# Moving two VectorE operations later in each step of a cross-attention and routing pipeline

## The reference

```python
# x: (32, 100, 256), ctx: (32, 361, 192)
x1 = layernorm(layernorm(x)) * g1 + b1            # two norms in a row
x2 = layernorm(ctx) * g2 + b2
q, k, v = x1 @ Wq + bq, x2 @ Wk + bk, x2 @ Wv + bv
attn = softmax(q @ k.T * E ** -0.5)               # row maximum subtracted
x = x + (attn @ v) @ Wo + bo

h = layernorm(x)                                  # 3200 tokens
shared = gelu(h @ ws1 + bs1) @ ws2 + bs2
aff = softmax(h @ Wr + br)                        # 31 experts
vals, idx = top_k(aff, 3)
routed = sum over the 3 experts e of vals_e * (gelu(h @ We1[e] + Be1[e]) @ We2[e] + Be2[e])
x = x + shared + routed + h
```

## Time and profile before

| | us |
|---|---|
| median of 3 runs | 512.76 |
| lowest, highest | 511.71, 514.05 |
| the profiled execution | 512.76 |
| its span | 511.0 |

### The profile page before, as it was taken

How to read it: one execution, slowest core, us unless ns; L and a number is a source line. 1 busy time by engine, 2 the same in 40 slices (tenths; PEclk the granted TensorE clock), 3 DMA queues, 4 the chain that set the end, 5 groups by cost and what they waited for, 6 DMA issues and landing times.

```text
span 511.0 us, 13549 instructions
## 1 busy us (share of the span) xinstructions
PE 461.7 (90%) x3204; PEld 407.2 (80%) x3204; DVE 350.6 (69%) x1556; ACT 247.2 (48%) x821; POOL 324.9 (64%) x363
## 2 busy tenths in 40 slices
PE   1899888889798989988899999999999999999992
PEld 1777777778677778767799889999999999999891
DVE  4747878887878887657467666666666666661684
ACT  1255655556465654656355454555554545552220
POOL 6123756857576755747078888888888888885000
PEclk9989999999999997999999999999999999999997
DMA  7374876767575972568369999998888888875999
GB/s 242 101 215 126 243 224 196 247 206 244 182 236 175 347 250 75 192 212 314 97 133 181 187 189 182 182 153 140 137 136 140 135 139 135 138 115 79 331 349 325
DMA packets 80621, 97.53 MB, mean 191 GB/s; under 512 B 8689, under 2 KB 65298, under 8 KB 80546
## 3 DMA queue, kind: packets, MB, share of 16 engines
q1 hardware_dynamic: 60786, 70.79, 45.8%
q0 software_dynamic: 19472, 25.61, 30.0%
q10 hardware_dynamic: 288, 0.27, 0.3%
HBM read 54.91 MB, written 41.73 MB: 189 GB/s over the span
## 4 chain that ended last, share of the span: by engine, by line
PE 45%; DVE 16%; DMA 9%; issue 9%; POOL 5%; SPq 4%; ACT 2%; POOLq 0%; DVEq 0%
PE bank L1184 12%; PE bank L1195 11%; DMA sum<-y_sb,token 7%; PE bank L1173 3%; DVE w_all L732 3%; POOL sum L557 2%; PE bank L1085 2%; PE bank L1086 2%; DMA w_all<-sum 2%; PE bank L1039 2%; PE bank L1051 2%; PE bank L1040 1%; SPq L449 1%; DVE c L695 1%; DVE y_sb L790 1%
## 5 line engine op out<-in xcount | busy, mean ns | idle before, releaser
L557 POOL DMA_INDIRECT sum<-y_sb,token x105 | 170.3, 1622 | 47.3 <-issue 24.6
L643 ACT ACTIVATE up<-bank,b_all 128x128 f32<-128x128 f32 x260 | 81.4, 363 | 102.0 <-PE bank L1184 65.8
L1184 PE MATMUL bank<-xtt,w1b 128*128 128x128 f32 x840 | 111.1, 275 | 0.3 <-ACT xtt L669 0.3
L1195 PE MATMUL bank<-w_all,up 128*128 x420 | 108.5, 381 | 0.0
L1184 PEld LDWEIGHTS bank<-xtt,w1b 128*128 128x128 f32 x840 | 102.1, 192 | 0.7 <-ACT xtt L669 0.5
L921 DVE TENSOR_SCALAR y_sb<-bank,gate,inverse 128x256 f32<-128x256 f32 x105 | 57.1, 544 | 55.1 <-PE bank L1195 54.9
L535 POOL DMA_INDIRECT expert_rows_in<-xt,slot x75 | 76.2, 1016 | 21.0 <-issue 20.7
L1195 PEld LDWEIGHTS bank<-w_all,up 128*128 128x128 f32 x420 | 71.7, 191 | 5.7 <-issue 0.2
L913 DVE COPY w1b<-w_all 128x512 f32 x105 | 47.8, 455 | 16.7 <-PE bank L1184 5.9
L669 ACT ACTIVATE xtt<-bank 128x256 f32<-128x256 f32 x105 | 40.1, 383 | 38.7 <-PE bank L1173 38.1
L1173 PE MATMUL bank<-ident,xt 128*128 128x128 f32 x210 | 40.1, 273 | 0.3 <-DMA xt<-expert_rows_in 0.3
(11 more groups left out here) (180 smaller groups left out, 935.4 us busy)
## 6 DMA issues: line engine op xcount, KB each, us to landing
xt<-expert_rows_in SPq DMA_DIRECT2D x105, 132.0 KB
w_all<-in_w SPq DMA_DIRECT2D x47, 256.0 KB, 5.0
w_all<-in_ctx SPq DMA_DIRECT2D x32, 288.0 KB, 3.0
w_all<-sum SPq DMA_DIRECT2D x15, 384.0 KB, 7.5
sum<-pad_rows SPq DMA_DIRECT2D x1, 3328.0 KB, 12.7
w_all<-in_x SPq DMA_DIRECT2D x25, 128.0 KB, 3.3
sum<-y_sb SPq DMA_DIRECT2D x25, 128.0 KB, 3.5
sum<-xt SPq DMA_DIRECT2D x25, 128.0 KB, 3.4
```

The source lines that it names most:

```text
L557: pool.indirect_dma_start(sums[s], bass.IndirectOffsetOnAxis(ap=token[sx][:, 0:1], axis=0), y_sb[sx][:, :], None, compute_op=ALU.add).then ...
L643: ins = act.activation(up[s][:, m * P:m * P + P], up_ps[s][:, m * P:m * P + P], ACT.Gelu, bias=b1_all[:, e, m:m + 1].rearrange("p o n -> p ...
L1184: mm = pe.matmul(up_ps[s][:, m * P:m * P + P], w[:, c * INTER + m * P:c * INTER + m * P + P], xtt[s][:, c * P:c * P + P], start=(c == 0), ...
L1195: mm = pe.matmul(down_ps[s], up[s][:, m * P:m * P + P], w, start=(m == 0), stop=(m == 1))
```

## The change

Two pieces of VectorE's `step` change their place; no instruction is added, removed or altered, and no semaphore either. The three `bn_stats` of the context stood first in the step and now stand behind the reciprocal L700 and the logit sum L706. The row maximum stood ahead of `picks`; now it stands behind `mask` and ahead of the reciprocal L782.

```diff
@@ -689,11 +689,6 @@
                 new, met, rated = batch(i + 2), batch(i + 1), batch(i - 1)
                 new_x, met_x = starts(i + 2), starts(i + 1)
                 mixed, added_t, routed, gated = ends(i - 2), ends(i - 3), ends(i - 4), ends(i - 5)
-                if new is not None:
-                    dve.wait_ge(c_in[new % SLOTS], (new // SLOTS + 1) * 16)
-                    for k in range(3):
-                        ins = dve.bn_stats(c6[new % 2][:, k, :], c_sb[new % SLOTS][:, k, :])
-                    ins.then_inc(ctx_stat6, 1)
                 if gated is not None:
                     s = gated % 2
                     dve.wait_ge(meta_made, gated + 1)
@@ -704,6 +699,11 @@
                     if routed >= 2:
                         dve.wait_ge(meta_made, routed - 1)
                     dve.tensor_tensor(rec[r2][:, 0:NE], logit_ps, br_s[:, :], ALU.add).then_inc(logit_sum, 1)
+                if new is not None:
+                    dve.wait_ge(c_in[new % SLOTS], (new // SLOTS + 1) * 16)
+                    for k in range(3):
+                        ins = dve.bn_stats(c6[new % 2][:, k, :], c_sb[new % SLOTS][:, k, :])
+                    ins.then_inc(ctx_stat6, 1)
                 if gated is not None:
                     s = gated % 2
                     dve.wait_ge(rsum_made, gated + 1)
@@ -748,10 +748,6 @@
                 if new_x is not None:
                     dve.wait_ge(x_in[new_x % 8], (new_x // 8 + 1) * 16)
                     dve.bn_stats(x6[new_x % 2][:, :], x_sb[new_x % 8]).then_inc(x_stat6, 1)
-                if rated is not None:
-                    s = rated % 2
-                    dve.wait_ge(scores_made, rated + 1)
-                    dve.tensor_reduce(negmax[s][:, :], bank[s][0:LQ, 0:LK], AX.X, ALU.max, negate=True).then_inc(rowmax_made, 1)
                 if routed is not None:
                     dve.wait_ge(idx_float, routed + 1)
                     dve.tensor_tensor(picks[r2][:, :, :], iota_e[:, :].unsqueeze(1).to_broadcast([P, TOP, NE]),
@@ -776,6 +772,10 @@
                     with nc.allow_low_precision(reason="zeros and ones"):
                         dve.tensor_reduce(mask[r2][:, :], picks[r2][:, :, :].rearrange("p k e -> p e k"), AX.X,
                                           ALU.add).then_inc(mask_made, 1)
+                if rated is not None:
+                    s = rated % 2
+                    dve.wait_ge(scores_made, rated + 1)
+                    dve.tensor_reduce(negmax[s][:, :], bank[s][0:LQ, 0:LK], AX.X, ALU.max, negate=True).then_inc(rowmax_made, 1)
                 if mixed is not None:
                     m2, m4 = mixed % 2, mixed % SLOTS
                     dve.wait_ge(attn_made, mixed + 1)
```

## The result

| | us |
|---|---|
| before, median of 20 runs (lowest, highest) | 513.74 (511.25, 515.82) |
| changed, median of 20 runs (lowest, highest) | 518.25 (512.55, 522.11) |
| ratio | 1.0058, 95% interval 1.0031 to 1.0087 |
| the changed kernel's profiled execution, its span | 518.9, 517.1 |

The change makes the kernel slower by 0.3 to 0.9%. 514.2 was forecast, a loss of 0.3%, in a range of 509.0 to 518.0. The ratio puts the changed kernel at 515.7 (1.0058 times the 512.76 that the forecast started from), inside the range; the median of its 20 runs, 518.25, is just above it. The spread of the runs has doubled, which is the first hint.

The account below looks back on a forecast made before the run. No engine bounds the steps throughout; VectorE or TensorE sets the pace. Start +1.2, two rounds +0.4, steps 27 to 31 +0.1, step 32 -0.3: +1.4 on 511.0, plus 1.8 around the span, 514.2 us; range 509.0 to 518.0.

Parts of the forecast that it names:

- the ledger: Sum of K shifts over the steps: about 2.1 us won at `mask` per round, all spent at L1091; 514.2 us, chance 0.48.
- The mask's gain: On VectorE, the row maximum no longer stands ahead of `mask`, so `mask` comes 0.44 us sooner.
- K: Start of the rank product (L1080) on TensorE, which `mask` releases; the forecast counts each step's shift there.
- The cost at the logit product: TensorE's L1091 waits for ScalarE's copy L616 behind the later maximum: 0.38 us late with output products, 1.04 without.
- Step 18's wait at L1091: TensorE's logit product can't start before K+1.39 instead of K+1.01, 0.38 us late.
- The reciprocal's wait: VectorE's L700 newly waits about 1.6 us for ScalarE's record (L635), once or twice a round.
- the slower rival: ScalarE's record some 0.35 us later, or slower statistics, makes the reciprocal's wait set `mask`: 518.2 us, chance 0.20.
- The clock: TensorE's 2.01 us wait before K becomes 1.57, making the low-clock drop behind step 27, 2.1 us, less likely.
- The drop does not come: Rival: the TensorE low-clock stretch behind step 27 vanishes, 514.2-2.1 = 512.1 us, chance 0.22.
- Faster: Rival: the logit product L1091 does not hold TensorE, so `mask` keeps its 5.7 us gain: 507.0 us, chance 0.10.
- The statistics' move is in no sum: On VectorE, the statistics' move alone hides behind TensorE in every step, so no time was counted for it.

Follow-up runs that it names:

- the first set of experiments: Kernel before 513.0 us; against it the statistics' move alone 511.61 us (0.998), the maximum's move alone 521.44 us (1.0178).
- the third set: On another chip, kernel before 526.1 us; against it the changed kernel 527.28 us (1.0043), and with unread products in TensorE's waits 519.64 us (0.9909).
- the copy first: Both moves plus ScalarE's copy of the transposed tokens (L616) ahead of the exponentials, against the kernel before: 520.75 us, 0.9865.
- the second set: On another chip, kernel before 528.6 us; against it L616 ahead of the exponentials with both moves 520.75 us (0.9865), with the maximum's move alone 525.08 us (0.9923).
- the filled changed kernel: Changed kernel with 4, 3 and 3 unread products in TensorE's waits, against the kernel before: 519.64 us, 0.9909.

## Why the prediction was nearly right, and where it failed

**The direction held, and the ledger in its main terms.** The mask's gain: VectorE's wait before L782 is 0.84 us in step 18 where it was 1.27, and K of step 23 to K of step 24 is 6.72 us for 7.18, -0.46 (forecast -0.44). The cost at the logit product: K of step 24 to K of step 25 is 184.25-177.92 = 6.33 for 5.28, +1.05 (forecast +1.04). Step 18's wait at L1091 was there. The reciprocal's wait came at the forecast size and place:

```profile
180.56 0.17 DVE L695 RECIPROCAL rsum<-xt 128x1 f32<-128x1 f32 x1 [1.58 <-ACT xt L635]
180.74 0.87 DVE L705 BATCH_NORM_STATS2 c<-w_all 128x6 f32<-128x192 f32 x3
...
183.71 0.24 DVE L773 TENSOR_REDUCE mask<-picks 128x31 bf16<-128x93 f32 x1
```

`mask` at 183.71 is K+5.79 of step 24 (K+5.65 forecast) and is done before TensorE comes at 184.25. It had 0.24 us left (0.30 is needed before K), where 0.35 was forecast. So the slower rival, by the record, was rightly kept off the path.

That the round came out at +0.21, as in the ledger, is partly luck. Between K of step 19 and of step 20 the measured shift is -0.34 us (150.49-144.05 = 6.44 for 6.78) where the ledger has -0.04, from there to K of step 21 it is +0.98 (6.33 for 5.35) for +0.58, from step 21 to 23, less the drop, +0.07 for -0.09, and from step 25 to 27 -0.64 (12.52 for 13.16) for -0.44. These errors cancel.

**What failed is the step called "The clock".** It let one drop stand and made its vanishing the likelier surprise, on the argument that 2.01 us of waiting became 1.57 us. Two things are wrong in it. First, the wait shrank further, to 1.08, and the drop came in steps 9 and 18 nevertheless (in step 27 it did not). I had looked at one wait by itself and not at the new ones at L1091: 0.21 us close behind it in the same step, and 0.93 in step 22 (0.48 before), where the other drop fell. Which of the waits sets off a drop was not tested one by one. Second, I had priced no new drop at all. The runs of two comparisons, 21 executions of the changed kernel beside a kernel before at 513.74 us (the profiled one among them), and 29 of the kernel before in the first set of experiments, at 513.0 us, show how time and clock go together:

| | before | changed |
|---|---|---|
| median of the mean granted clock | 0.980 | 0.978 |
| time per 0.01 of mean granted clock, least squares | -2.1 us | -6.9 us |
| correlation | -0.68 | -0.96 |
| times at 0.984 | 511.6 (median of 4) | 513.7, 513.7, 516.2 |
| times at 0.977 | 513.1 (median of 6) | 518.8 to 520.3 (7 runs) |

So the kernels differ little in how much of the clock is lost, and more in how long they take when it is lost: the changed kernel is near 2 us behind at 0.984, where the ledger has 1.4, and near 6 at 0.977. The slope isn't the price of drops alone. A hundredth of the mean clock over 517 us is 5.2 us of clock lost. Every drop priced here costs less than it loses, so the changed kernel's 6.9 holds something else that comes with the drops; what that is stays open. The price itself is read from the profiles. Before, a stretch at 0.53 of 7.2 us lost 0.47*7.2 = 3.4 us of clock and cost 2.1 of time, 0.61 of it. After, (1-0.79)*8.16 = 1.7 us lost cost 1.43, and (1-0.75)*6.8 = 1.7 cost 1.52, 0.84 and 0.89. The two halves of the change separate this. Here is the stretch from K of step 27 to K of step 28, first with the statistics alone, then with the maximum alone:

```profile
190.08:197.91 7.83, 7.76 (x48) 6.72 (x49) 5.88 (x30) 3.41 (x16) 5.38 (x10) 0.78 0.29 89
```

```profile
198.42:206.59 8.17, 7.96 (x48) 6.29 (x49) 6.31 (x31) 4.00 (x17) 5.72 (x10) 0.79 0.29 89
```

Both lose 1.7 us of clock. With the statistics alone that costs 7.83-7.14 = 0.69 us, by a stretch without a drop in the same profile; with the maximum alone 8.17-6.73 = 1.44, by the changed kernel's. Where VectorE sets K, a slow TensorE eats its own idle first. The maximum's move spent that idle. In the third set the changed kernel also loses more clock than before (medians 0.968 against 0.974); why that differs from chip to chip stays open.

**The rivals.** "The drop does not come" has the sign wrong. "Faster" is refuted by L1091's 9.5 us, and its condition was tried by itself: with the copy first, the time was 1.35% below the kernel before in the second set, but waits for the exponentials and for L785 at the start of the next step took the place of L1091's, which the rival hadn't named. "The statistics' move is in no sum": by itself it changes nothing that can be measured, but beside the maximum's move it seems to help by up to 1.2% (1.0178 against 1.0058, in different comparisons, drops included). 0.3 us a round is explained above. The rest goes with the clock: the six runs of the maximum alone have granted clocks of 0.968 to 0.975, and at such clocks the changed kernel's own least-squares line gives 520.6 to 525.4 us, where they took 519.6 to 526.5. Why the maximum alone loses more of the clock stays open.

**The size.** The term that was too small is that of the clock. Forecast +1.4 us. Measured: 3.0 us by the ratio, 6.1 in the profiled executions. Two rounds with 2.95 us of drops each, less the 2.1 of the drop that the kernel before had, are +3.8; with the ledger's 1.4 that is 5.2 against 4.3 at the end of the steps. The remaining -0.9 is about the changed execution's earlier start (the first reciprocal L782 at 38.13 us for 38.91); I take that for a matter of the loading ahead of the steps and not of the change, which is not shown.

## What to carry to other kernels

An idle stretch of the engine with the variable clock isn't only time to be won: while it lasts, it pays for slow clock stretches. An edit that trades it one for one against another wait can look neutral in a ledger at full clock and still lose. So price the low level too: take a stretch of the trace at either level, and ask which engine would then be late. And when an operation is moved behind the one that others wait for, follow its own reader's queue to the end: here an exponential on ScalarE had a copy behind it for which TensorE waited.

## What the runs showed of the hardware that I had not expected

Filling TensorE's waits with products that nobody reads made a kernel faster, 519.64 for 527.28 us on one chip. A float32 product of 128 columns took 0.22 us of TensorE, two instructions of 0.11 in the trace. The same kernel took 513.0, 526.1 and 528.6 us in three sets on three chips, with median granted clocks of 0.980, 0.974 and 0.969; in the slower two, ScalarE and TensorE show waits that the profile puts down to "issue" or "remote" and that the first chip's profiles lack in the steps, as before the second line here, from the filled changed kernel of the third set:

```profile
151.00 0.91 PE L1018 MATMUL bank<-fold_q 128*128 128x128 f32 x6
152.33 0.63 PE L1102 MATMUL bank<-wr_s,tok 128*128 128x31 f32 x4 [0.42 <-issue]
```
